# The first pair of tiles counted beside the second half of the first layer's messages

## What is computed

```python
for l in range(2):
    x_res = x
    h = x @ W[l]
    msg = norm[:, None] * h[src]
    agg = jax.ops.segment_sum(msg, dst, num_segments=N) + b[l]
    x = jax.nn.relu(agg + x_res @ resW + resb)
```

## Time and profile before

| | |
|---|---|
| median of 3 runs | 1909.43 us (1906.18 to 1910.65) |
| the profiled execution | 1904.65 us, of which the span from first to last instruction is 1902.9 us |
| mean granted TensorE clock | 0.984 of full speed |
| PE busy | 1817.4 us (96%), DVE 1124.6 (59%), ACT 853.9 (45%), POOL 341.2 (18%) |
| DMA | 416.70 MB, 219 GB/s in the mean |

### The profile page before, as it was taken

The page is one execution under the profiler, slowest core; times in us unless marked ns, Lnnn a source line. Parts: engine busy times, 40 slices in busy tenths (PEclk is TensorE's granted clock), DMA queues, the critical chain, the costliest instruction groups (busy, mean ns, idle before and its releaser), DMA issues. The chain is left out here.

```text
span 1902.9 us, 35412 instructions
## 1 busy us (share of the span) xinstructions
PE 1817.4 (96%) x11170; PEld 1119.2 (59%) x11170; DVE 1124.6 (59%) x2789; ACT 853.9 (45%) x1822; POOL 341.2 (18%) x347
## 2 busy tenths in 40 slices
PE   4787999999999999999999999999999999999996
PEld 3576555555555555555544444444444478888885
DVE  7787666766666666666514444444444567555553
ACT  2366565656555565655512222222222232556562
POOL 1582000000000000000001111111111124333332
PEclk9898999999999999999999999999999999999998
DMA  7257999898999999985285544444445479324441
GB/s 235 76 118 151 327 299 333 294 293 267 319 259 309 276 364 320 363 311 198 104 341 183 188 183 179 179 179 179 179 180 185 177 236 331 112 76 122 140 139 52
DMA packets 135978, 416.70 MB, mean 219 GB/s; under 512 B 13685, under 2 KB 81611, under 8 KB 129640
## 3 DMA queue, kind: packets, MB, share of 16 engines
q1 hardware_dynamic: 90376, 255.13, 38.2%
q0 software_dynamic: 45392, 160.65, 27.9%
q10 hardware_dynamic: 144, 0.13, 0.0%
HBM read 162.27 MB, written 262.07 MB: 223 GB/s over the span
## 5 line engine op out<-in xcount | busy, mean ns | idle before, releaser
L1404 PE MATMUL bank<-parts,counts 128*128 128x512 f16 x4704 | 1157.8, 379 | 0.9 <-DVE sums L1425 0.9
L1404 PEld LDWEIGHTS bank<-parts,counts 128*128 128x128 f16 x4704 | 415.9, 97 | 357.9 <-issue 2.5
L1559 ACT ACTIVATE counts<-bank 128x392 f16<-128x392 f32 x800 | 394.8, 497 | 314.8 <-PE bank L1479 308.0
L623 DVE TENSOR_TENSOR rows<-rows,iota_lo 128x2048 bf16<-128x2048 bf16 x200 | 245.0, 1225 | 236.0 <-PE bank L1479 235.5
L1479 PEld LDWEIGHTS bank<-rows 128*128 128x128 bf16 x3200 | 229.6, 99 | 204.5 <-issue 27.4
L1479 PE MATMUL bank<-rows 128*128 128x98 bf16 x3200 | 280.5, 212 | 11.7 <-DVE rows L623 10.9
L623 DVE TENSOR_TENSOR rows<-rows,iota_hi 128x1568 bf16<-128x1568 bf16 x200 | 193.7, 968 | 0.0
L467 POOL DMA_INDIRECT first_rows<-route_rows,route_spot_i x49 | 47.8, 976 | 604.5 <-DVE tokens L458 405.0
L1419 ACT ACTIVATE middle<-bank 128x256 f32<-128x256 f32 x98 | 37.1, 380 | 186.8 <-PE bank L1404 172.1
L2187 PE MATMUL bank<-y_t,counts 128*128 128x256 f32 x480 | 115.3, 384 | 3.3 <-ACT y_t L2259 3.3
L2187 PE MATMUL bank<-h_t,counts 128*128 128x256 f32 x480 | 113.7, 380 | 0.0
(11 more groups left out here) (268 smaller groups left out, 1764.0 us busy)
## 6 DMA issues: line engine op xcount, KB each, us to landing
counts_table<-counts SPq DMA_DIRECT2D x25, 3136.0 KB, 15.1
counts<-counts_table SPq DMA_DIRECT2D x24, 3136.0 KB, 11.6
first_rows<-zero_rows POOLq DMA_DIRECT2D x3, 10530.0 KB, 57.6
second_rows<-zero_rows POOLq DMA_DIRECT2D x3, 10449.0 KB, 66.4
first_out<-zero_rows POOLq DMA_DIRECT2D x3, 10368.0 KB, 49.1
res_tile<-res_table SPq DMA_DIRECT2D x98, 128.0 KB, 7.1
first_rows<-zero_rows POOLq DMA_DIRECT2D x1, 10270.0 KB, 58.0
second_rows<-zero_rows POOLq DMA_DIRECT2D x1, 10191.0 KB, 63.2
```

The costliest lines, as they stand in the source:

```text
L623: return nc.vector.tensor_tensor(rows, k, v, ALU.is_equal)
L1404: mm = nc.tensor.matmul(acc[:, 0:2 * dim], lhs, rhs, start=s == 0, stop=s == tiles)
L1559: nc.scalar.activation(counts[:, b, :, :].rearrange("p s (o n) -> p o s n", o=2)[:, :, :, q * QUAD:(q + 1) * QUAD], bank[4 + q % 4][:, 0:Q ...
```

## The change

The counts of pair 0 are made in the prologue, beside the message loop from tile 25 on, where the first half of `feat` is no longer read. The layer program no longer makes them; it opens with 12 sums of pair 0 (`SUMS_AHEAD`) and then goes on as before with pair 1's quads beside the other 88.

- PE: after `message(t)`, for t from 25 to 46, `count_quad(q)` for one or two quads (`quads_after(t)`: 32 quads over 22 tiles). They use two banks, 6 and 7; from the third quad on each waits until the quad two before it is copied out.
- ACT: in iteration t, after `high(t)`, `middle(t-1)` and the copy of keys, `quad_copy(q)` for the quads of tile t-1.
- DVE: after `rest_of(t)`, one of eight low one-hots (`pair_heads`) at t = 15, 17, 28, 31, 34, 36, 39 and 42, and the tile one-hot (`pair_tiles`) one tile later.
- The matmul that sums the disorder flags moves from bank 6 to bank 5, and waits for the copy of the keys there.
- In the layer program DVE and ACT start with pair 1; SP stores the counts of pair 0 as soon as they are complete, as before.

```diff
+        FREE_AFTER = -(-tiles // 2)
+        COUNT_FOR = tiles - FREE_AFTER - 2
+
+        def quads_after(t):
+            return range(*(min(max(n, 0), COUNT_FOR) * quads // COUNT_FOR for n in (t - FREE_AFTER, t + 1 - FREE_AFTER)))
+
+        def quad_bank(q):
+            return bank[6 + q % 2]
+
+        ONEHOTS_AFTER_H = (15, 17) + tuple(FREE_AFTER + -(-(r - 1) * per_step * COUNT_FOR // quads) for r in range(2, steps))
...
             def _(act):
+                def quad_copy(q):
+                    act.wait_ge(quad_ready, q + 1)
+                    nc.scalar.activation(
+                        counts[:, 0, :, :].rearrange("p s (o n) -> p o s n", o=2)[:, :, :, q * QUAD:(q + 1) * QUAD],
+                        quad_bank(q)[:, 0:QUAD * width].rearrange("p (n o s) -> p o s n", o=2, s=tiles), ACT.Copy).then_inc(quad_out, 1)
...
                     if t in (9, 17, 27):
                         roots(2 + (9, 17, 27).index(t))
+                    for q in quads_after(t - 1):
+                        quad_copy(q)
...
             def _(pe):
+                def count_quad(q):
+                    r, u0 = divmod(q * QUAD, STEP)
+                    if u0 == 0:
+                        pe.wait_ge(onehots_made, r + 1)
+                    if q >= 2:
+                        pe.wait_ge(quad_out, q - 1)
+                    for u in range(QUAD):
+                        at = (u0 + u) // 2
+                        mm = nc.tensor.matmul(quad_bank(q)[:, u * width:(u + 1) * width], pair_lo[:, r % 2, at, :, u % 2],
+                                              pair_hi[:, r % 2, at, :, u % 2], start=True, stop=True)
+                    mm.then_inc(quad_ready, 1)
...
                     if t == FLAG_AFTER_H:
                         pe.wait_ge(disorder_ready, 1)
-                        nc.tensor.matmul(bank[6][:, 0:3], ones[:, :], disorder[:, :], start=True, stop=True).then_inc(ones_summed, 1)
+                        pe.wait_ge(keys_out, pairs - 1)
+                        nc.tensor.matmul(bank[5][:, 2 * P:2 * P + 3], ones[:, :], disorder[:, :], start=True, stop=True).then_inc(ones_summed, 1)
+                    for q in quads_after(t):
+                        count_quad(q)
...
             def _(dve):
+                def pair_heads(r):
+                    if r == 0:
+                        dve.wait_ge(keys_out, 1)
+                        dve.wait_ge(consts_made, 4)
+                    if r >= 2:
+                        dve.wait_ge(quad_ready, (r - 1) * per_step)
+                    onehot_rows(pair_lo[:, r % 2, :, :, :], keys_t[:, 0, 1, r * STEP:(r + 1) * STEP], iota_lo, STEP, P)
+
+                def pair_tiles(r):
+                    onehot_rows(pair_hi[:, r % 2, :, :, :], keys_t[:, 0, 0, r * STEP:(r + 1) * STEP], iota_hi, STEP, width).then_inc(onehots_made, 1)
...
                     if t == 24:
                         overflow()
+                    if t in ONEHOTS_AFTER_H:
+                        pair_heads(ONEHOTS_AFTER_H.index(t))
+                    if t - 1 in ONEHOTS_AFTER_H:
+                        pair_tiles(ONEHOTS_AFTER_H.index(t - 1))
                     if t == 37:
                         flag_and_bounds()
...
+        SUMS_AHEAD = 12
...
                 def sum_pair(i, b, first, last=False):
                     pe.wait_ge(quad_out, i * quads + quads)
                     units = LAST_UNITS if last else UNITS
+                    ahead = SUMS_AHEAD if first else 0
+                    if first:
+                        sum_units(pe, b, i, i, 0, ahead, update.sums_out, update.sums_ready, first)
                     for q in range(quads):
                         if not last:
-                            build(q, i + 1, False)
-                        sum_units(pe, b, i, i, q * units // quads, (q + 1) * units // quads, update.sums_out, update.sums_ready, first,
+                            build(q, i + 1)
+                        sum_units(pe, b, i, i, ahead + q * (units - ahead) // quads, ahead + (q + 1) * (units - ahead) // quads, update.sums_out, update.sums_ready, first,
                                   chunk_free=chunk_free if last else None)
...
-                for q in range(quads):
-                    build(q, 0, True)
                 sum_pair(0, 0, True)
```

More of the change, by code:

```diff
@@ L608, in rows_of @@
             return table.rearrange("(t p) d -> p t d", p=P)
+        QUAD = 4
+        quads = P // QUAD
+        STEP = 16
+        steps = P // STEP
+        per_step = STEP // QUAD
         open_scope()
@@ L664, in gnn_moe_kernel @@
         assert 2 * pairs % BATCH == 0 and BATCH % 2 == 0
+        pair_lo = sb("pair_lo", [P, 2, STEP // 2, P, 2], BF16)
+        pair_hi = sb("pair_hi", [P, 2, STEP // 2, width, 2], BF16)
         windows = onehot_lo[:, :, :, :, :].rearrange("p b s v j -> p (b s v j)").bitcast(I32)[:, 0:2 * pairs * slots].rearrange("p (t s) -> p t s", s=slots)
@@ L727, in gnn_moe_kernel @@
         middle_ready = sem("middle_ready")
+        onehots_made = sem("onehots_made")
+        quad_ready = sem("quad_ready")
+        quad_out = sem("quad_out")
         HEAD_STEPS = head_cols // HIST
@@ L811, in _ @@
                 nc.gpsimd.tensor_scalar(odd, odd, -float(tiles), None, ALU.add).then_inc(consts_made, 1)
-                nc.gpsimd.iota(iota_hi[:, :, :], [[1, width], [0, 2]], 0, 0, allow_small_or_imprecise_dtypes=True)
+                nc.gpsimd.iota(iota_hi[:, :, :], [[1, width], [0, 2]], 0, 0, allow_small_or_imprecise_dtypes=True).then_inc(consts_made, 1)
                 link(nc.gpsimd.tensor_copy(ident_h[:, :], ident[:, :]))
@@ L1135, in flag_and_bounds @@
                     dve.wait_ge(ones_summed, 5)
-                    link(nc.vector.tensor_reduce(over[:, 0:1], bank[6][:, 0:3], AX, ALU.add))
+                    link(nc.vector.tensor_reduce(over[:, 0:1], bank[5][:, 2 * P:2 * P + 3], AX, ALU.add))
                     link(nc.vector.tensor_scalar(over[:, 0:1], over[:, 0:1], 1.0, None, ALU.min))
@@ L1383, in _ @@
                         nc.vector.tensor_tensor(gs_agg[:, :], gs_agg[:, :], bank[1][:, 0:dim], ALU.add).then_inc(column_made, 1)
-        QUAD = 4
-        quads = P // QUAD
         UNITS = 2 * (tiles + 1)
         LAST_UNITS = tiles + 1
+        SUMS_AHEAD = 12
         half_bank = 2
@@ L1453, in count_and_sum @@
             keys_copied = sem("keys_copied")
-            onehots_made = sem("onehots_made")
-            quad_ready = sem("quad_ready")
-            quad_out = sem("quad_out")
             counts_stored = [sem(f"counts_stored{b}") for b in range(2)]
-            STEP = 16
-            steps = P // STEP
-            per_step = STEP // QUAD
             keys = carve([P, 2, 2, P], BF16)
@@ L1469, in tensor, with build @@
             def tensor(pe):
-                def build(q, i, first):
+                def build(q, i):
                     r, u0 = divmod(q * QUAD, STEP)
@@ L1474, in build @@
                         pe.wait_ge(onehots_made, i * steps + (r + 1))
-                    if not (first and q < 4):
-                        pe.wait_ge(quad_out, i * quads + (q - 3))
+                    pe.wait_ge(quad_out, i * quads + (q - 3))
                     for u in range(QUAD):
@@ L1509, in vector, with rows_of_step @@
             def vector(dve):
-                def rows_of_step(r, i, b, first):
-                    if not (first and r < 2):
-                        dve.wait_ge(quad_ready, i * quads + (r - 1) * per_step)
+                def rows_of_step(r, i, b):
+                    dve.wait_ge(quad_ready, i * quads + (r - 1) * per_step)
                     nodes_of = slice(r * STEP, (r + 1) * STEP)
@@ L1524, in pair @@
                                           keys_t[:, bass.ds(i, 1), :, :].rearrange("p a k n -> p (a k n)")).then_inc(keys_copied, 1)
-                    dve.wait_ge(keys_copied, i + 1)
+                    dve.wait_ge(keys_copied, i)
                     for r in range(steps):
-                        rows_of_step(r, i, b, isinstance(i, int) and i == 0)
+                        rows_of_step(r, i, b)
                         if there(i * 2 - 4):
@@ L1542, in pair @@
                                 update.res_and_message(dve, i * 2 - 2, 0, i - 1)
-                for i in range(4):
+                for i in range(1, 4):
                     pair(i, i % 2)
```

## The result

| | |
|---|---|
| median after | 1934.97 us (1932.81 to 1939.35) |
| median before, run beside it | 1908.46 us |
| ratio after / before | 1.0143, 95% interval 1.0129 to 1.0156 |
| the profiled execution | 1939.35 us, span 1937.0 us |
| mean granted TensorE clock | 0.972 |

The change makes the kernel 26.5 us slower. The prediction said 1928, within 1913 to 1950, slower with a chance of 0.86. Direction and size are right; the mechanism behind them is right in its shape and wrong in one respect, the clock. The 26.5 lie even inside the bounds that the forecast gave for a clock that stays at 1.00 (12 to 29), though the clock fell. That is in part luck: other terms erred the other way.

What follows compares the result with a forecast made beforehand. PE, DVE and ACT each idle in the message loop, so its chain was read as its pace; PE is full from 194 us. Added 39.1 less 19.0 saved gave 20.1 us longer: 1928 us, range 1913 to 1950.

Steps and rivals of the forecast that it cites:

- The ring closes in one tile: In message tiles 27 to 46, all but tile 37, the next message waits for a quad copy of the same tile.
- Its length: One message tile, from message over `high`, `middle`, quad copy and quad to the next message: 2.83 us, bounds 2.50 to 3.14.
- The clock stays at 1.00: In the slow message tiles PE, busy about 1.4 of 2.83 us, keeps full speed, as at 103 to 106 us.
- The rival: The clock falls in the slow message tiles: 1.05 us more a tile over 19 tiles, about 1948 us; chance 0.12.
- The early one-hots: DVE's added one-hots at tiles 15 to 18 delay message 27 by 1.6 us, bounds 0 and 2.6.
- The tail: From message 47 to the last `middle`: 4.1 us instead of 3.4, so 0.7 more.
- The saving at the program's start: The first sum moves to the layer program's start: 19.0 us saved, bounds 16.6 and 19.1.
- The gap of 3.2 us as a fixed cost: Between message loop and layer program nothing runs for 3.2 us (leaving the block, the flag, the branch), before and after.
- The other signs: New profile: first sum within 0.5 us of DVE's first copy, pair 1's quads not waiting for one-hot rows, loop ending near 211.
- the sums behind the opening: In the layer program the sums are only reordered; the new opening pays the slow first 3.4 us of sums too, once.

Runs made afterwards that it cites:

- the run with the copies ahead: The changed kernel with the quad copies of the tile before put ahead of `high` in ACT's iteration: 1900.44 us, ratio 0.9982.
- the fillers: The changed kernel with ten matmuls that nothing reads after each message of tiles 27 to 46: 1923.26 us, ratio 1.0101.
- the flag cut up: The changed kernel with quad copies ahead of `high` and the flag's DVE chain cut into two links a tile from tile 36: 1896.80 us, ratio 0.9942.

## Why the prediction was right, and where it was not

- **The ring closes in one tile: right.** The order of the links is in both timelines above, and the run with the copies ahead shows that it sets the time: with the same work in another order, 1.0143 becomes 0.9982.
- **Its length: one link too long.** At full clock it is 2.54 us (with PE kept busy) where the prediction had 2.83, just inside its bounds. The mis-sized link is that from the quad to the next message, put at 0.47 (0.36 for the quad and 0.11 of lag): it measured 0.20. The quad's 0.36 in the earlier trace rows is from one group's first weight load to the next group's; here the message's weights load while the quad still runs. At full clock the loop would have grown by 32.6 us, not 36.8.
- **The clock stays at 1.00: wrong.** This is the step that failed. The prediction argued from the residual loop, where PE kept 1.00 in a ring with ACT; here the granted clock fell at tile 31, was back at 1.00 in tile 32, and was 0.50 from tile 33 to the end of the loop. It cost 13.9 us. That it goes with PE's waits is shown by the fillers, which kept it at 1.00 in the same ring; what tells this ring apart from the residual loop's stays open. One row at 1.00 was thin ground: in five of the thirteen profiles the residual loop itself lost the clock for some us (last section). The rival's price of 1.05 a tile was right (3.60 less 2.54 is 1.06); its base of 2.83 was too long, and it counted 19 slow tiles where 15 were. The rule of the Trainium skill that the prediction weighed ("TensorE: Matmul & The Clock Gate", section "A second HAM failure mode: psum-queue depth-cycling") was borne out by the trace in that the clock was lost in a loop that cycles through banks and idles shortly between. It describes a clock that swings between the two levels; here it swung once (down near 165 us, up near 169, down near 172) and then stayed at 0.50 for over 50 us.
- **The early one-hots: too small.** 2.8 us, where I took 1.6 with bounds of 0 and 2.6. At tile 24 it was 2.3 (`high(0)` to `high(24)` 28.10 us, before 25.81), so most of DVE's delay was passed on, and the slack I gave PE and the four banks was hardly there. The other 0.5 came in tiles 25 to 27, where the first two quads and their copies stand: a term that the prediction put at nothing.
- **The tail: too small.** 1.8 instead of 0.7, as messages 47 and 48 run at half clock.
- **The saving at the program's start: right,** 19.0 us.
- **The gap of 3.2 us as a fixed cost: wrong.** It was mostly a wait for GpSimd's loads, which two runs with the loads moved show. In the changed kernel the loop outlasts the loads, and 2.3 us come back. The other side of it is that the kernel before gained nothing from a shorter loop (0.9998).
- **The other signs.** The first sum came as foretold, and pair 1's quads did not wait for one-hot rows. The loop ended at 226.9, not near 211.

In one sum, on the profiled executions: of the 34.1 us between the spans 4.0 were there before the message loop began, so 30.1 belong to the change, where the prediction had 20.1. The loop is 9.7 above its term (13.9 for the clock, less 4.2 for the ring), the early one-hots 1.2, the tail 1.1, the sums behind the opening 1.1, the gap 2.3 below: 10.8 in all, 0.8 more than the spans show. Without the fall of the clock the sum of 20.1 would thus have been some 3 us too high. The run with PE kept busy, whose clock didn't fall, is 19.0 above the kernel before in the medians and 16.6 in the profiled executions from `high(0)` on. Why the medians of the changed kernel differ by only 26.5, and not by 30, was not tried.

## What to carry to other kernels

Before adding work to a loop over several engines, write down for each new wait which iteration of the other engine releases it, and what stands ahead of the releasing instruction there: a copy two places further down in ACT's list made a tile 2.5 us instead of 1.6 to 1.8, and in the slow tiles the clock fell as well. When such a ring is found, try first to move the releasing instruction to the front of its iteration. That needs no buffer and opened the ring in nearly every tile here, while a third bank was free from tile 33 on only. And before a loop is shortened, look at what else has to be done by its end. Here the loads held the layer program back: the shorter loop gained nothing while they did, and moving them gained 0.15%. That the shorter loop gains beside this is seen in the start of the program (2.1 us) and not in the medians.

## What the runs showed of the hardware

- PE lost its clock in a ring of 2.8 us a tile (1.00 in the tile at 159.94, then down, up and down again between 165 and 172, then 0.50 to the end of the loop). Ten short matmuls more in each tile kept it at 1.00, and where a third bank opened the ring it came back to 1.00 (180 to 185 us).
- A pause of PE was followed by either level. Behind one of 2.85 us (copies ahead) and one of 3.03 (third bank) it was 0.50; with the flag cut up, without the pause, it stayed at 1.00. Near 95 us, in the residual loop, PE pauses for 2.85 to 3.04 us in all thirteen profiles: in eight the clock is 1.00 behind it, in five it is 0.50 from 98 to 100 us.
- The layer program's first instruction came 4.7 to 4.9 us after the last packet of GpSimd's queue; with all loads in earlier it came 0.97 to 0.98 us after the loop's last instruction.
- Up to the message loop the profiled executions differ, though the change adds nothing there: `high(0)` starts between 118.8 and 120.5 us in eight of the kernels, at 122.65 in one, and between 123.9 and 124.3 in four, both profiles of the changed kernel among these. From 80 to 118 us the granted clock is 1.00 in the kernel before and 0.91 in the changed one. The five later ones are those whose clock fell behind the pause near 95 us, as the matmuls behind it show, in the kernel before and in the changed one. Some 1.1 us of the 4.0 are there already at that point. Why the clock fell in these five was not tried.

```profile
96.57 1.13 PE L941 MATMUL bank<-both_w,counts 128*128 128x256 f32 x4 [3.02 <-ACT counts L861]
```
```profile
97.70 2.07 PE L971 MATMUL bank<-both_w,counts 128*128 128x256 f32 x4 [3.02 <-ACT counts L883]
```
